# Local attention in a decoder kernel: 64-row score products instead of spread queries

## What is computed

```python
q, k = l2norm(q) * q_scale, l2norm(k) * k_scale
q, k = rotary_xpos(q, k)                 # q*cos*scale + rotate_half(q)*sin*scale, k with /scale
bq = q.reshape(b, h, w, WINDOW, d) * QK_SCALE            # QK_SCALE = 8
sim = jnp.einsum('bhwid,bhwjd->bhwij', bq, look_around(bk))
mask = (i < j) | (i > j + WINDOW) | (j == -1)
sim = jnp.where(mask, -jnp.finfo(sim.dtype).max, sim)
attn = jax.nn.softmax(sim, axis=-1)
out = jnp.einsum('bhwij,bhwjd->bhwid', attn, look_around(bv))
```

## Time and profile before

| what | value |
|---|---|
| median of 3 executions | 4002.15 us (4001.81, 4002.15, 4016.12) |
| the profiled execution | 4016.23 us |
| its span, first to last instruction | 4014.5 us |
| TensorE, VectorE, ScalarE, GpSimd busy over the span | 77%, 54%, 38%, 18% |
| mean granted TensorE clock, share of full speed | 0.887 |
| the four calls of `local_attention` | 77.56, 78.07, 78.68 and 77.57 us |

### The profile page before, as it was taken

How to read it: one execution, slowest core, us unless ns; L and a number is a source line. 1 busy time by engine, 2 the same in 40 slices (tenths; PEclk the granted TensorE clock), 3 DMA queues, 4 the chain that set the end, 5 groups by cost and what they waited for, 6 DMA issues and landing times. The chain is left out here.

```text
span 4014.5 us, 51524 instructions
## 1 busy us (share of the span) xinstructions
PE 3109.4 (77%) x16845; PEld 1899.8 (47%) x16853; DVE 2164.0 (54%) x5116; ACT 1524.2 (38%) x4242; POOL 713.3 (18%) x735
## 2 busy tenths in 40 slices
PE   6585785755999998566976888988879867768993
PEld 3563443232666665333743654436543444445762
DVE  6437455353777774779934664236632555652223
ACT  4212464222776674430033442224421125632331
POOL 2201001011111110002503451024510111211113
PEclk9686998877999999787988999999999979978997
DMA  1000002010000000000000000000000000040112
GB/s 59 1 1 0 13 1 69 0 36 20 1 1 1 1 2 20 32 11 0 1 14 28 1 1 30 0 28 1 1 29 0 16 19 1 1 189 28 33 33 72
DMA packets 34785, 80.09 MB, mean 20 GB/s; under 512 B 8577, under 2 KB 23698, under 8 KB 30450
## 3 DMA queue, kind: packets, MB, share of 16 engines
q1 hardware_dynamic: 28738, 63.04, 4.3%
q0 software_dynamic: 4368, 11.93, 1.1%
q10 hardware_dynamic: 1440, 2.12, 0.1%
HBM read 63.05 MB, written 14.02 MB: 19 GB/s over the span
## 5 line engine op out<-in xcount | busy, mean ns | idle before, releaser
L2201 PE MATMUL psum<-XT,Q_heads 128*128 128x512 f32 (+3 forms) x768 | 299.2, 499 | 3.0 <-POOL Q_heads L2178 2.8
L2263 DVE TENSOR_SCALAR zero_marks<-psum 128x128 f32<-128x128 f32 (+7 forms) x256 | 192.1, 750 | 107.4 <-PE psum L2202 105.3
L2282 ACT ACTIVATE scores<-scores,min 128x128 f32<-128x128 f32 (+7 forms) x256 | 198.4, 775 | 86.1 <-DVE min L2265 82.7
L2265 DVE CUSTOM_DVE_ANT_0 scores<-psum,zero_marks 128x128 f32<-128x128 f32 (+7 forms) x256 | 194.1, 758 | 29.6 <-issue 0.5
L2209 PE MATMUL psum<-ident,scores 128*128 128x128 f32 x1152 | 175.1, 280 | 21.1 <-ACT probsT L2299 17.4
L2299 ACT ACTIVATE probsT<-psum 128x128 f32<-128x128 f32 (+7 forms) x256 | 162.8, 636 | 70.2 <-PE psum L2209 69.8
L651 PE MATMUL psum<-ident,probs 128*128 128x128 f32 (+1 forms) x768 | 118.4, 277 | 81.0 <-ACT probs L757 81.0
L3481 PE MATMUL psum<-Hn,W 128*128 128x512 f32 x384 | 168.7, 602 | 9.2 <-PEq L394 9.2
L3365 ACT ACTIVATE probs<-psum,stat 128x256 f32<-128x256 f32 (+1 forms) x256 | 115.5, 458 | 131.0 <-DVE stat L3329 130.9
L2209 PEld LDWEIGHTS psum<-ident,scores 128*128 128x128 f32 x1152 | 125.3, 142 | 84.1 <-issue 54.3
L2201 PEld LDWEIGHTS psum<-XT,Q_heads 128*128 128x128 f32 x768 | 129.6, 196 | 73.7 <-issue 65.2
(11 more groups left out here) (610 smaller groups left out, 7205.7 us busy)
## 6 DMA issues: line engine op xcount, KB each, us to landing
W<-in_L3f_W SPq DMA_DIRECT2D x16, 1024.0 KB, 21.9
L3f_y_rows<-y SPq DMA_DIRECT2D x39, 128.0 KB, 1.7
L0f_rows<-Xtok SPq DMA_DIRECT2D x2, 2048.0 KB, 8.8
W<-in_L0f_W SPq DMA_DIRECT2D x3, 1152.0 KB
Wqkv<-in_L2f_Wqkv SPq DMA_DIRECT2D x2, 1536.0 KB, 8.5
W<-in_L2f_W SPq DMA_DIRECT2D x2, 1536.0 KB
XT<-in_xT SPq DMA_DIRECT2D x1, 2048.0 KB, 7.8
Xtok<-in_xtok SPq DMA_DIRECT2D x1, 2048.0 KB, 13.0
```

Source lines behind the costliest of these rows:

```text
L2201: pe.matmul(sc(i)[:, o:e], Qh[:, u % 2, h, :], KT[:, c, b * S + o:b * S + e], start=True, stop=(e < n), skip_group_check=True)
L2263: dve.tensor_scalar(zero[:, i % 2, 0:n], sc(i)[:, 0:n], 0.0, -NEG, ALU.is_equal, ALU.mult)
L2265: dve.tensor_tensor_reduce(Sc[:, i % ROT, 0:n], sc(i)[:, 0:n], zero[:, i % 2, 0:n], 1.0, -NEG, ALU.add, ALU.min, low[:, i % ROT:i % ROT + ...
L2282: act.activation(p, p, ACT.Exp, bias=low[:, i % ROT:i % ROT + 1], scale=-1.0, accum_out=sums[:, u % 2, h:h + 1]).then_inc(s["exp_done"], 1)
```

## The change

Heads of a pair are scored from their own 64 partitions of `QT` and `KT`; the head `hh` = 0 of two pairs goes to one PSUM bank and `hh` = 1 to another. So a half `G` of a tile (pairs 2G and 2G+1, four heads) fills banks 2G and 2G+1, and one bfloat16 product per bank adds the mask for two heads, 512 columns wide (two of 128 columns in tile 0). The queries are no longer spread. The factor -8 goes into the query half of the rotation table, so scores come out negated: the mask is negated, the maximum becomes a minimum, its scaling goes, and the exponential has scale -1. Reciprocals are taken for four heads at once. TensorE's order for a tile is now S0, t0, t1, S1, t2, t3, value products, where S0 and S1 score half a tile; ScalarE's is exponentials of S0, copy of turn 1, exponentials of S1, copy of turn 3.

```diff
-def local_attention(nc, K, b, QT, KT, V, half, window_mask, OT):
+def local_attention(nc, K, b, QT, KT, V, window_mask, OT):
-        Qh = sbuf(es, nc, "Q_heads", [P, 2, LM, 2, P])
+        pairs_of = lambda G: (2 * G, 2 * G + 1)
...
-            def score(t, g):
-                if g == 0:
-                    pe.wait_ge(s["q_spread"], 2 * (t + 1))
+            def score(t, G):
+                ks = keys(t)
                 if t:
-                    pe.wait_ge(s["exp_done"], LH * (t - 1) + 2 * (g + 1))
+                    pe.wait_ge(s["exp_done"], LH * (t - 1) + 4 * (G + 1))
+                for g in pairs_of(G):
+                    for hh in range(2):
+                        own = slice(hh * LHD, (hh + 1) * LHD)
+                        pe.matmul(K.bank[2 * G + hh][:, (g % 2) * 2 * P + ks.start:(g % 2 + 1) * 2 * P], QT[own, g, t * P:(t + 1) * P],
+                                  KT[own, g, t * P - P + ks.start:(t + 1) * P], start=(g % 2 == 0), stop=False, skip_group_check=True)
                 for hh in range(2):
-                    ks = keys(t)
-                    o = K.bank[g][:, hh * 2 * P + ks.start:(hh + 1) * 2 * P]
-                    pe.matmul(o, Qh[:, t % 2, g, hh, :], KT[:, g, t * P - P + ks.start:(t + 1) * P], start=True, stop=False, skip_group_check=True)
-                    ins = pe.matmul(o, K.identb[:], window_mask[:, ks], start=False, stop=True, skip_group_check=True)
-                ins.then_inc(s["scored"], 1)
+                    if t:
+                        ins = pe.matmul(K.bank[2 * G + hh][:], K.identb[:], window_mask[:], start=False, stop=True, skip_group_check=True)
+                    else:
+                        for half in range(2):
+                            ins = pe.matmul(K.bank[2 * G + hh][:, half * 2 * P + P:(half + 1) * 2 * P], K.identb[:], window_mask[:, ks],
+                                            start=False, stop=True, skip_group_check=True)
+                    ins.then_inc(s["scored"], 1)
...
-                for g in range(LM + 1):
-                    if g < LM and t + 1 < NTB:
-                        score(t + 1, g)
-                    if g:
-                        turn(t, g - 1)
+                for G in range(HALVES):
+                    if t + 1 < NTB:
+                        score(t + 1, G)
+                    for g in pairs_of(G):
+                        turn(t, g)
...
         def _(dve):
-            def spread(t): ...
+            def minima(t, G):
+                if G == 0 and t >= 2:
+                    dve.wait_ge(s["exp_done"], LH * (t - 1))
                 for hh in range(2):
+                    dve.wait_ge(s["scored"], 2 * (HALVES * t + G) + hh + 1)
+                    dve.tensor_reduce(stat[:, t % 2, 0, 4 * G:4 * G + 4].rearrange("p (g hh) -> p hh g", hh=2)[:, hh, :],
+                                      K.bank[2 * G + hh][:].rearrange("p (h k) -> p h k", h=2)[:, :, keys(t)], AX, ALU.min).then_inc(s["min_done"], 1)
...
             for t in range(NTB):
+                minima(t, 0)
+                if t:
+                    take_turned(LM * (t - 1))
+                minima(t, 1)
+                recip(t, 0)
                 if t:
                     take_turned(LM * (t - 1) + 2)
+                recip(t, 1)
                 if t:
+                    take_out(t - 1)
...
-                act.wait_ge(s["max_done"], LM * t + g + 1)
...
                 for hh in range(2):
+                    act.wait_ge(s["min_done"], 2 * (HALVES * t + G) + hh + 1)
+                    for g in pairs_of(G):
...
+                                       scale=-1.0, accum_out=stat[:, t % 2, 1, h:h + 1]).then_inc(s["exp_done"], 1)
...
             for t in range(NTB):
-                for g in range(LM):
+                for G in range(HALVES):
                     if t + 1 < NTB:
-                        exps(t + 1, g)
+                        exps(t + 1, G)
+                    take_turned(LM * t + 2 * G + 1)
...
-        block_mean(nc, K, ones64[:], LHD)
         block_mean(nc, K, J[:], P)
...
+                for i, mask in enumerate((K.below, K.above, K.below, K.above)):
+                    dve.tensor_scalar(wm[:, i * P:(i + 1) * P], mask[:], -1.0, None, ALU.mult)
...
+                            dve.tensor_scalar(sc[:, 0:2, :], sc[:, 0:2, :], -QK_SCALE, None, ALU.mult)
+                            dve.drain()
                             for i in range(4):
                                 dve.tensor_tensor(tab[:, i], tab[:, i], middle(sc[:, i, :], S // P), ALU.mult)
```

More of the change, by code:

```diff
@@ L3084 @@
 WINDOW = 128
+QK_SCALE = 8.0
 def xpos_tables():
@@ L3230, in _ @@
                 pool.tensor_tensor(t1[:, n % 2], t1[:, n % 2], inner(r[:, n % 2], LHD), ALU.mult).then_inc(s["normed"], 1)
-def local_attention(nc, K, b, QT, KT, V, half, window_mask, OT):
+def local_attention(nc, K, b, QT, KT, V, window_mask, OT):
     NTB = S // P
-    QK_SCALE = 8.0
-    with ExitStack() as es, phase(nc, K.sems, "q_spread scored max_done exp_done recip_done normed turned pt_out_even pt_out_odd pv_done out") as (block, s):
-        Qh = sbuf(es, nc, "Q_heads", [P, 2, LM, 2, P])
+    HALVES = LM // 2
+    with ExitStack() as es, phase(nc, K.sems, "scored min_done exp_done recip_done normed turned pt_out_even pt_out_odd pv_done out") as (block, s):
         Pr = sbuf(es, nc, "probs", [P, 2, LH, 2 * P])
@@ L3309, in take_turned, with take_out @@
                 dve.tensor_copy(dst, src).then_inc(s["pt_out_even"], 1)
-            spread(0)
+            def take_out(t):
+                dve.wait_ge(s["pv_done"], LM * (t + 1))
+                dve.tensor_copy(OT[:, :, b * S + t * P:b * S + (t + 1) * P], K.bank[6 + t % 2][:].rearrange("p (g k) -> p g k", g=LM)).then_inc(s["out"], 1)
             for t in range(NTB):
[L3313 to L3333, removed]
@@ L3368, in _ @@
-            for g in range(LM):
-                exps(0, g)
+                    act.wait_ge(s["min_done"], 2 * (HALVES * t + G) + hh + 1)
+                    for g in pairs_of(G):
+                        h = 2 * g + hh
+                        c0 = (g % 2) * 2 * P
+                        act.activation(Pr[:, t % 2, h, ks], K.bank[2 * G + hh][:, c0 + ks.start:c0 + ks.stop], ACT.Exp, bias=stat[:, t % 2, 0, h:h + 1],
+                                       scale=-1.0, accum_out=stat[:, t % 2, 1, h:h + 1]).then_inc(s["exp_done"], 1)
@@ L3370, in _, with take_turned @@
+            def take_turned(n):
+                act.wait_ge(s["turned"], n + 1)
+                if n >= LM:
+                    act.wait_ge(s["pv_done"], n - LM + 1)
+                src, dst = turned_probs(n)
+                act.activation(dst, src, ACT.Copy).then_inc(s["pt_out_odd"], 1)
+            for G in range(HALVES):
+                exps(0, G)
             for t in range(NTB):
-                for g in range(LM):
+                for G in range(HALVES):
                     if t + 1 < NTB:
-                        exps(t + 1, g)
[L3374 to L3380, removed]
+                        exps(t + 1, G)
+                    take_turned(LM * t + 2 * G + 1)
@@ L3409, in L2_ffn @@
         sh = sbuf(es, nc, "shifted", [P, B, 1 + S])
-        half = sbuf(es, nc, "head_half", [P, 2])
-        ones64 = sbuf(es, nc, "ones64", [P, P])
         J = sbuf(es, nc, "J", [P, P])
-        wm = sbuf(es, nc, "window_mask", [P, 2 * P], BF16)
-        block_mean(nc, K, ones64[:], LHD)
+        wm = sbuf(es, nc, "window_mask", [P, 4 * P], BF16)
         block_mean(nc, K, J[:], P)
```

37 lines of the change are left out of this document (12 added, 25 removed).

## The result

The changed kernel takes 3952.3 us (3947.7 to 3955.6, four runs) against 4005.5 for the kernel before (four runs: the three of the table ahead and one more); the ratio is 0.9854, interval 0.9837 to 0.9870. That is 53 us less; 47 were forecast, and 3955 as the time. In a second comparison on another chip it was 3955.0 against 4010.9 (seven runs), 56 us less, ratio 0.9869 (0.9849 to 0.9890).

A forecast was written before the change was run, and what follows sets the result against it. TensorE's queue plus one wait for ScalarE was taken as the bound. Four calls gave -46.7 us and the fixed part -0.6, total -47.3, from a median of 4002.15 to 3955; range 3938 to 3988.

The forecast's parts named there:

- Full overlap: Score products: the 64-row passes of a pair's two heads run together, 4 slots of 0.215 us for half a tile.
- serial rival: Score products: 64-row passes run one after the other, a tile takes 9.57 us, the program 4005, no change; chance 0.13.
- in-part rival: Score products: passes pair only at borders of heads, 5 slots instead of 4, tile 8.34 us, program 3967; chance 0.12.
- The new chain: Steady tile followed from scores through ScalarE's copies to the last value products: next tile at 7.91 us, 1.42 gained.
- Changes of shape: TensorE in a tile: three more switches between product shapes, 0.15 us each; ends 0 and 0.4 each.
- Neither is late: VectorE and GpSimd in a tile: neither holds up the chain; VectorE holds 5 us, GpSimd 4.16 of work.
- (a): Start of a call: no wait for spreads and half the score slots, -1.8 us.
- (b): Tile 1 to tile 2 of a call: 9.44 us becomes 8.1, with half clock at first, -1.35.
- (c): Tile 2 to 3 of a call: 10.84 us with a half-clock stretch of 3.4 left in place, -1.42.
- (d): Five further tiles of a call: -7.1 us.
- (e): Tail of a call, last turns and value products: unchanged.
- Clock rival: TensorE's granted clock drops to half because of waits and half-filled rows: 4114 us at half clock throughout; chance 0.06.

The follow-up runs named there:

- e1: Changed kernel with each score product over all 128 rows instead of the head's own 64: 3989.0 us, ratio 0.9949 to the kernel before; steady tile 9.15 us.
- e2: Changed kernel with the score products of a half tile issued head by head instead of pair by pair: 7.85 us a tile, calls 64.0 to 64.9.
- e6: Changed kernel with the copy of turn 3 moved from ScalarE to VectorE: 3939.9 us, ratio 0.9832 to the kernel before; 7.44 us a tile.
- e9: Changed kernel plus two unused VectorE copies from PSUM per tile, scores waiting for those of the tile before: 7.84 to 7.85 us a tile, calls sum 259.1.
- e7: Changed kernel with all four copies of turned probabilities on VectorE, only exponentials on ScalarE: 3932.7 us, ratio 0.9808 to the kernel before; 7.17 us a tile.
- e4: Changed kernel with VectorE again making the two unused spread copies, scores waiting for them: tiles of 7.95 and 8.26 us in turns, calls sum 269.3.
- e3: Kernel before with only the factor -8 folded into the rotation table, minima instead of maxima, no scaling: 8.88 us a tile, calls sum 291.6.
- e5: Changed kernel plus two unused VectorE copies from PSUM, scores mistakenly waiting for those of the tile just finished: 8.78 us a tile, calls sum 287.1.

## Why the prediction was right

*Score products.* Full overlap was taken, on the ground of the value products. It holds: 1.06 us to the mask was forecast, 1.06 measured, and e1 measures the other end, 1.73. The serial rival said that a tile would take 9.57 with the shape changes; e1, which has none, takes 9.15. The in-part rival, 8.34, fell with the result: its five slots would have given 1.28 to the mask. e2, where the written order leaves still less to pair (seven slots, 1.7), takes 1.07.

*The new chain.* Forecast against measured from the tile's start: first minimum 1.53 and 1.57, first exponential 2.25 and 2.38, S1 2.5 and 2.48, its first exponential 4.75 and 4.78, turn 3 at 4.83 and 4.94, value products 5.33 and 5.50, copy of turn 3 at 6.6 and 6.59, last pair 7.31 and 7.25, next tile 7.91 and 7.84. That ScalarE's copy is what is late next is shown by e6, where it goes and 0.40 us a tile with it. The wait ahead of turn 3, which I had listed as well, costs nothing while that copy is later; e6 still has it (0.35), and e7, which takes the copy of turn 1 off ScalarE too, is a further 0.27 shorter.

*Changes of shape.* Taken as 0.15 each. The passes of S0 start 0.215 apart from 0.32 on, so they end at 0.96, and the mask starts at 1.06: 0.1 to leave, as read from the value products. e1, whose scores have the shape of the mask's product, loses nothing at that place. Nothing like the 0.4 of the upper end. The Trainium skill (TensorEngine Tiling (Array Packing), Key Properties) says that a change of tiling mode drains the engine; the trace agrees, with 0.1 us as its size.

*VectorE.* "Neither is late" was right for its time (e9). But the chain of the forecast is that of a kernel without spreads and scalings, and beyond the start of a call nothing in it says what these two removals are worth. Had the spreads stayed in the new order, they would have cost 12.9 us (e4): 4 x 1.0 at the starts of the calls, most of the rest by meeting GpSimd, which the old trace had not shown in a steady tile.

*A call.* In the first call: (a) The start: -1.8 forecast, 5.40 - 3.65 = -1.75 measured. (b) Tile 1 to 2: 9.44 went to 7.19, -2.25 instead of -1.35. (c) Tile 2 to 3: 10.84 went to 7.84, -3.0 instead of -1.42. (d) Five tiles: -7.4 instead of -7.1. (e) The tail: 5.3 both times. Sum -14.4. The first call is the best of the four. As means of all four the terms are -2.1, -1.6, -2.5, -7.4 and 0, sum -13.6, where -11.7 was forecast. More than half of the difference is (c), the half-clock stretch "I leave there": it is gone from all four calls. The windows view of the first call, split just ahead of the scores of tile 1, and behind it tile 1 of the second call (the last but two number is the granted clock):

```profile
2228.60:2232.11 3.51, 3.45 (x24) 2.57 (x24) 0.95 (x3) 2.72 (x9) 0.00 (x0) 0.51 0.01 5
2232.12:2291.76 59.64, 53.69 (x500) 38.23 (x500) 35.07 (x70) 35.99 (x137) 30.59 (x32) 1.00 0.01 1
...
2355.27:2363.63 8.36, 7.21 (x44) 4.15 (x44) 4.18 (x12) 5.91 (x26) 4.26 (x6) 0.81 0.00 0
```

In the first call half clock ends before tile 1, where (b) had counted some. In the other three it reaches into tile 1 (granted 0.78 to 0.81), which takes 8.4 to 8.7 there; the 8.1 of (b) lies between. No second stretch follows in any of the four, where (c) had a dip: tile 2 to 3 takes 7.84 in all of them, and took 9.8 to 10.8 before. The fold alone (e3) already does without that dip, at 8.88; e4 has it in one call and e5 in three. What in the first tiles decides it was not tried and stays open.

*Clock rival.* Half-filled rows did not lower the clock: 1.00 in a steady tile, with 7.32 us busy of 7.84, and 0.97 over the first call, above the 0.93 to 0.95 that was named as a sign.

*Fixed part.* The phase for `ones64` is gone (-1.2). The scaling of the table costs 0.31 ahead of the four multiplications, as taken. The spans of the two profiled executions differ by 64.3 us, 9.9 more than the calls. Of these, 3.5 lie ahead of this sublayer (its first VectorE instruction comes 4.7 us earlier, of which 1.2 is the phase) and 3.3 behind its last call, in code that did not change. That is the spread between executions, the reason why medians are compared.

*Luck.* The time came out 2.7 us from the forecast, closer than the working earns. The saving was forecast 6 us too small, 47 against 53; the kernel before measured 4005.5 where the forecast started from 4002.15, and that gave 3.4 of the 6 back.

## What to carry to other kernels

Two small products that use different rows and different banks ran together at full worth here, in whatever order they were written; padding an operand with zeros to fill the array cost twice, in TensorE slots and in the engine that pads. Follow the new chain to its end before stopping: here it ended in a copy that stood behind exponentials on one engine while another was idle, and moving that copy gave 15 us more, and moving the one ahead of it as well 22, for no change of the arithmetic. And price a removed operation by how many of it lie in series in the chain, not by how many there are, and an added or kept one by what the other engines do at its place in the new order: what held a tile up here was not the two spreads' 0.8 us but their meeting with GpSimd.

## What the runs showed of the hardware

Passes of two heads in different rows start together, pair by pair. TensorE's timeline of the changed kernel's tile, cut off at 2279.00 and at 2279.16:

```profile
2278.62 0.70 PE L3263 MATMUL psum<-KT,QT 64*128 64x256 f32 x4
...
2278.62 0.92 PE L3263 MATMUL psum<-KT,QT 64*128 64x256 f32 x6
```

Four passes have begun by the first moment and six by the second, and the end moves by 0.22, the slot of one full-row pass of 256 columns. Head-by-head order gives the same (e2), although there four passes of one head are written ahead of the other's. The Trainium skill (TensorE: Matmul & The Clock Gate, Part 3) has products of different rows run together, and the trace agrees; that they keep the written order in start and end, by which e2 would take 1.7 us to the mask, does not fit its 1.07.

A VectorE multiplication of 128x512 float32 from and to SBUF took 0.475 us alone and up to 1.27 beside a GpSimd multiplication. It waited: all 25 spreads of e4 that took over 0.5 us ended 0.28 us behind the end of the GpSimd multiplication that was at work when they began, however long that had run (2252.84 against 2252.56, and 2244.89 against 2244.60, in the rows of e4). By contrast, a copy of 128x512 from PSUM took 0.66 us beside it (turn 2 at 2276.04 in the changed kernel, GpSimd from 2276.20 on) and 0.68 without it (turn 0 at 2281.39, GpSimd done at 2280.24), and the copies of 128x256 from PSUM in e9 took 0.42 to 0.43 with GpSimd at work. The Trainium skill (SBUF — State Buffer, Who interferes with whom) has it that a `tensor_scalar` or a copy from and to SBUF can work in a mode that takes the port pair shared with GpSimd, which whoever issues first holds for the whole instruction, and that an operation with at most one SBUF input outside those modes does not meet GpSimd; e4 and e9 agree.
